# DLRM tower on one core: weight loads of the cross stage moved from SyncE's queue to ScalarE's

## The reference, cut to what matters

```python
q1, q2 = attention_pool(x, w1, b1, w2), attention_pool(x, w3, b3, w4)     # softmax over the 50 fields
h = concat([q1, q2]) @ w5 + b5                                            # 300 numbers
f6 = h @ w6 + b6
iu, ju = triu_indices(300, k=1)                                           # 44850 pairs
f7 = (h[:, iu] * h[:, ju] * g) @ w7 + b7                                  # w7 is 44850 x 300: the cross stage
out8 = concat([f6, f7]) @ w8 + b8
z = einsum('bu,bku->bk', out8, label_embedding)                           # 200 dot products a row
y = relu(relu(concat([z, dense_ctx]) @ W_top1 + b1) @ W_top2 + b2) @ W_top3
```

## Time and profile before

| | |
|---|---|
| median of 3 runs | 1852.51 us (1850.72 to 1853.8) |
| the profiled execution | 1854.63 us, its span 1852.8 us |
| TensorE busy | 1690.2 us, 91% of the span |
| VectorE busy | 1666.4 us, 90% |
| ScalarE busy | 1028.8 us, 56% |
| GpSimd busy | 554.8 us, 30% |
| moved by DMA | 561.70 MB, 303 GB/s on the mean |
| granted TensorE clock | 0.963 of full speed |

### The profile page before, as it was taken

How to read it: one execution, slowest core, us unless ns; L and a number is a source line. 1 busy time by engine, 2 the same in 40 slices (tenths; PEclk the granted TensorE clock), 3 DMA queues, 4 the chain that set the end, 5 groups by cost and what they waited for, 6 DMA issues and landing times.

```text
span 1852.8 us, 26080 instructions
## 1 busy us (share of the span) xinstructions
PE 1690.2 (91%) x7084; PEld 1249.0 (67%) x7084; DVE 1666.4 (90%) x5850; ACT 1028.8 (56%) x3233; POOL 554.8 (30%) x413
## 2 busy tenths in 40 slices
PE   2788899999999999999999999999997999998751
PEld 1555567777777777777777777777775777775531
DVE  5998979989999889999999999999998888867676
ACT  3786684684466644466654664456653544454434
POOL 7777506827300135400077018500000000000053
PEclk8899999999999999999999999999998999998975
DMA  9488955757988688989768766997649999989975
GB/s 277 114 290 316 340 181 189 244 169 278 380 320 308 238 325 350 353 333 342 288 223 337 272 253 216 385 418 295 247 163 396 421 390 378 401 311 419 420 304 242
DMA packets 97054, 561.70 MB, mean 303 GB/s; under 512 B 15567, under 2 KB 15941, under 8 KB 71309
## 3 DMA queue, kind: packets, MB, share of 16 engines
q1 hardware_dynamic: 77629, 498.39, 69.7%
q0 software_dynamic: 19264, 61.64, 10.5%
q10 hardware_dynamic: 16, 0.00, 0.0%
HBM read 559.98 MB, written 0.00 MB: 302 GB/s over the span
## 4 chain that ended last, share of the span: by engine, by line
PE 54%; DVE 23%; DMA 10%; POOL 6%; issue 4%; ACT 2%; SPq 0%; DVEq 0%; ACTq 0%; POOLq 0%
PE acc L1000 47%; DVE junk L618 11%; DMA w_sb<-in_w 8%; DVE qa L660 6%; DVE prod L770 6%; POOL x L561 4%; PE coarse L849 2%; DMA lab<-in_labels 2%; POOL lab L561 2%; PE acc L915 1%; PE misc L922 1%; PE acc L896 1%; PE acc L899 1%; ACT waste L1120 1%; PE acc L881 1%
## 5 line engine op out<-in xcount | busy, mean ns | idle before, releaser
L1000 PE MATMUL acc<-w_sb,prod 128*128 128x300 f32 (+2 forms) x5648 | 1528.1, 421 | 58.8 <-DMA w_sb<-in_w 41.3
L1000 PEld LDWEIGHTS acc<-w_sb,prod 128*128 128x128 f32 (+2 forms) x5648 | 1043.2, 192 | 405.7 <-DMA w_sb<-in_w 51.8
L1225 ACT ACTIVATE prod<-prod,g_all 128x256 f32<-128x256 f32 (+4 forms) x1615 | 686.3, 470 | 465.9 <-DVE prod L770 463.5
L561 POOL DMA_INDIRECT x<-in_tbl,ids_sb x368 | 477.7, 1298 | 664.9 <-DVE qa L660 558.9
L770 DVE TENSOR_TENSOR prod<-fine,coarse 128x1280 f32<-128x1280 f32 (+4 forms) x325 | 423.3, 1308 | 102.9 <-PE coarse L849 100.9
L618 DVE SCALAR_TENSOR_TENSOR junk<-lab,heads 128x300 bf16<-128x300 f32 x1208 | 477.6, 461 | 12.7 <-DMA lab<-in_labels 12.2
L618 DVE SCALAR_TENSOR_TENSOR junk<-x,heads 128x300 bf16<-128x300 f32 x1128 | 445.2, 461 | 24.0 <-DMA x<-in_tbl,ids_sb 23.9
L660 DVE SCALAR_TENSOR_TENSOR qa<-x,ex,qa 128x300 f32<-128x300 f32 x612 | 275.6, 523 | 0.0
L592 POOL TENSOR_TENSOR x<-x,out 128x2400 f32<-128x2400 f32 x5 | 26.2, 5253 | 599.9 <-ACT out L1095 591.1
L1120 ACT ACTIVATE waste<-x 128x300 bf16<-128x300 f32 x368 | 161.8, 440 | 26.4 <-DMA x<-in_tbl,ids_sb 25.1
L1044 ACT ACTIVATE picked<-hh 128x256 f32<-128x256 f32 (+4 forms) x325 | 121.6, 375 | 0.0
(11 more groups left out here) (107 smaller groups left out, 518.9 us busy)
## 6 DMA issues: line engine op xcount, KB each, us to landing
w_sb<-in_w SPq DMA_DIRECT2D x320, 750.0 KB, 6.6
lab<-in_labels SPq DMA_DIRECT2D x146, 1200.0 KB, 8.6
x<-in_labels SPq DMA_DIRECT2D x54, 1200.0 KB, 9.8
x<-in_tbl,ids_sb POOLq DMA_INDIRECT x368, 5.4
w_sb<-in_w SPq DMA_DIRECT2D x5, 450.0 KB, 3.7
prod<-in_v_i SPq DMA_DIRECT2D x1, 710.0 KB, 4.7
prod<-in_v_j SPq DMA_DIRECT2D x1, 710.0 KB, 7.1
w_sb<-in_w SPq DMA_DIRECT2D x1, 703.1 KB
```

The lines of the kernel that those rows point to most:

```text
L561: pool.indirect_dma_start(out=row_of(t, n), out_offset=None, in_=tables[n], in_offset=bass.IndirectOffsetOnAxis(ap=ids_sb[:, t, n:n + 1], ...
L1000: last = pe.matmul(acc[:, t % 3, 0:EMB], prod[0:rows, u % RING, m, t % 2 * P:(t % 2 + 1) * P], w7_sb[0:rows, u % W7_RING, m * EMB:(m + 1) ...
L1225: act.activation(chunk, chunk, ACT.Copy, scale=g_all[0:rows, pair:pair + 1]).then_inc(chunk_ready, 1)
```

## The change

The w7 loads of units 4 to 324 leave SyncE's list and are issued by ScalarE, on ScalarE's queue, one in each unit u from 2 to 322, right after the scaling of that unit's last chunk, for unit u + 2. Their wait (unit n - 4 used) goes with them. SyncE issues the first four w7 loads and then the slabs alone, in the same order among themselves, each with the wait it had. The sizes, `W7_RING` and `SLOTS` are as they were.

```diff
             for kind, n in LOADS:
                 if kind == "w7":
-                    if n >= W7_RING:
-                        sp.wait_ge(unit_used, n - W7_RING + 1)
-                    width = chunks_of(n) * EMB
-                    sp.dma_start(w7_sb[:, n % W7_RING, 0:width], w7[n % UNITS][:, 0:width]
-                                 ).then_inc(w7_loaded[n % W7_RING], 16)
+                    if n < W7_RING:
+                        sp.dma_start(w7_sb[:, n, :], w7[n]).then_inc(w7_loaded[n], 16)
                     continue
...
+            def load_w7(n):
+
+                width = chunks_of(n) * EMB
+                act.wait_ge(unit_used, n - W7_RING + 1)
+                act.dma_start(w7_sb[:, n % W7_RING, 0:width], w7[n % UNITS][:, 0:width]
+                              ).then_inc(w7_loaded[n % W7_RING], 16)
+
...
                     if m == 1 and u + RING < TOTAL:
                         pick_window(u + RING)
+                    if m == FINE - 1 and W7_RING <= u + 2 < TOTAL:
+                        load_w7(u + 2)
                     tick = u * FINE + m
```

## The result

The changed kernel takes 1855.97 us (median of 20 runs, 1852.52 to 1858.61), the kernel before 1853.18 (20 runs, 1849.52 to 1856.28). The ratio is 1.0017, with a 95% interval of 1.0010 to 1.0024. The forecast was 9.6 us faster. The predicted time of 1843 is 13 us off: the measured one lies above the forecast's own range of 1836 to 1850 and just inside the wide one of 1829 to 1857. The spans of the two profiled executions are 1856.2 and 1852.8 us, so the traces show about the same difference, 3.4 us.

The account below looks back on a forecast made before the run. TensorE (54% of the chain) and VectorE (23%) were taken to share the bound, with late data in places. Terms summed to -10.1, rounded to -9.6 from 1854.6: 1845.0, so median 1843; own range 1836 to 1850, wide 1829 to 1857.

Parts of the forecast that it names:

- the end stretch: Last cross units, DMAs full from 1645 to 1770 us: order of bytes changes nothing; 0, bounds -5 and +5.
- unit 247: Burst of six slabs: TensorE's 9.73 us wait for w7 shrinks, later slab 110 takes part back; -3.5, bounds 0 and -12.
- Unit 37: Four slabs ahead of w7: on its own queue w7 takes what gathers took, the 7.4 us wait goes; -8.
- (a): Head, 160 to 200 us: w7 beside the four earlier slabs lands late at two or three pairs; +1.5, bounds 0 and 6.
- (b): Around unit 37: four w7 issues by ScalarE, 0.33 us each, lie on the path; +1.3.
- The 2.4 us wait: One more TensorE wait for a w7 load behind a slab goes; -2.4.
- Elsewhere: Other units: w7, issued about one unit ahead, can be late behind a slab or two; +1, bounds 0 and 4.
- the change brings nothing: Rival, whole kernel: same bytes on the same engines, slabs lose what w7 gains; 1852.5 us, give or take 2; chance 0.20.

Follow-up runs that it names:

- late33: The changed kernel with slab 0 also waiting until unit 32 is used, so slabs 0 to 3 go out near 210 us: 1854.9 us, ratio 1.0016.
- order110: The changed kernel with slabs 110 and 111 issued ahead of the six slabs 112 to 117: 1843.1 us, ratio 0.9959.
- short_lead: The kernel before, one queue, with w7 of unit n also waiting until unit n - 2 is scaled, as late as in the change: 1875.2 us, ratio 1.0129.
- swap: Against the changed kernel, queues exchanged: SyncE issues w7 up to four units ahead, ScalarE most slabs, slabs 0 to 3 at units 33 to 36: 1875.1 us, ratio 1.0125.
- before_order: The kernel before, one queue, slabs 110 and 111 ahead of the six, those one behind each w7 of units 249 to 254: 1859.8 us, ratio 1.0045.
- one_queue: The kernel before with only its list reordered: slabs 0 to 3 later, 110 and 111 earlier, 112 onwards paced from unit 249: 1834.6 us, ratio 0.9898.

## Why the prediction was wrong, step by step

Three steps failed: the end stretch, put at 0 (+5.9), unit 247, put at -3.5 (+0.8), and the w7 loads beside the slabs in the head, put at +1.5 (the head lost 3.8 to 6.4, ScalarE's issues included). The rest held within 2 us.

- **Unit 37, -8**: right in size. The stage 36 to 45 is 8.3 us shorter. But by late33 the cause isn't the queue alone, since 5.2 us of waits stay beside the burst: the wait went mostly because the slabs moved off. The premise that w7 on its own queue takes what the gathers took, 7.1 to 9.1 us, failed there (up to 11.6): a gather moves 0.15 MB, a w7 load 0.77.
- **(a), +1.5 with bounds 0 and 6, and (b), +1.3**: under-sized. Unit 36 starts 6.4 us late (its cross 3.8 to 6.4 over the three traces with this head), and late33, with the slabs at 210, has its cross 0.7 late. The mechanism and the place were right: the first load beside a slab took 10.8 us from issue to landing where 7.1 are free. I took 8 at two or three pairs; four landings of 9.2 to 10.8 came with the first slab alone, beside the gathers and in a stretch already at 0.97. ScalarE's issue is 334 ns, as taken; that four of them lie on the path at unit 37 no run shows.
- **The 2.4 us wait**: measured -4.3, since the wait of before had also cost clock: 0.93 was granted in 1015 to 1040 before, 1.00 after. Before, then after:

```profile
1015.00:1040.00 25.00, 22.63 (x93) 16.67 (x92) 23.38 (x96) 14.34 (x47) 4.49 (x5) 0.93 0.87 346
```

```profile
1015.00:1040.00 25.00, 25.00 (x110) 18.93 (x109) 25.00 (x105) 19.98 (x66) 2.91 (x4) 1.00 0.92 344
```

- **Unit 247, -3.5 with bounds 0 and -12**: this step failed: +0.8. That slab 110 stays behind the six and holds VectorE was foreseen; its size was wrong. It took 20.1 us from issue to landing before and 25.9 after, 5.8 more instead of the 3.1 that I set. I had w7 of units 248 to 250 pass slab 110, "of which about two did not before". By the landings none did before, as they stood behind it in the queue (w7 248 landed at 1418.4, slab 110 at 1416.6), and all three do now (1404.9, 1409.6 and 1415.4 against 1418.6): 2.3 MB, 5.4 us at the 425 GB/s of that stretch, and the rate was 423 before (windows 1392.7 to 1418.6 and 1396.4 to 1416.5). And 3.1 was compared with absolute times: all of it came 3.7 us earlier in the changed kernel, so TensorE's 5.7 at unit 249 hold only 2.0 of gain from this place, and the next unit none. That unit 249 starts at 1423.9, close to the forecast 1424.9, is luck: the 3.7 were gained elsewhere. order110 shows that the 12 were there for another order. The three w7 loads in the changed kernel, and slab 110:

```profile
L1049 ACTq DMA_DIRECT2D w_sb<-in_w x3: 334/335/335, 1394.1 to 1406.2; - x3
...
DMA to landing us min/median/max: 9.1/10.7/11.0
```

```profile
L547 SPq DMA_DIRECT2D lab<-in_labels x1: 328/328/328, 1392.7 to 1392.7; - x1
...
DMA to landing us min/median/max: 25.9/25.9/25.9
```

- **The end stretch, 0 with bounds -5 and +5**: this step failed most: +5.9. "An order of bytes changes nothing where all of them are needed" left out that they needn't be moved inside the stretch. By the packets in the trace, the changed kernel enters unit 288 with one w7 load less landed (0.77 MB) and has 0.4 slabs more landed at unit 324: 55.0 MB instead of 53.8, or 2.9 us at 413 GB/s. The other 3.0 are rate, 404 against 413 GB/s, lost in the last 13.6 us: SyncE waits for free places there, and the DMAs run short. The windows of before, then after:

```profile
1640.20:1760.00 119.80, 100.10 (x387) 69.09 (x388) 89.71 (x368) 62.90 (x224) 0.00 (x0) 0.94 1.00 413
1760.00:1770.50 10.50, 8.31 (x33) 5.56 (x32) 8.54 (x39) 3.82 (x13) 0.00 (x0) 1.00 1.02 416
```

```profile
1637.40:1760.00 122.60, 96.90 (x386) 65.57 (x387) 90.02 (x366) 63.06 (x224) 0.00 (x0) 0.99 1.00 412
1760.00:1773.60 13.60, 8.90 (x34) 5.76 (x33) 9.62 (x45) 4.05 (x14) 0.00 (x0) 1.00 0.84 332
```

The step put this whole term at nothing. short_lead (one queue, short lead: 135.9) loses as much, with one w7 load more in the stretch, 0.2 slabs fewer, and 400 GB/s; swap (two queues, long lead: 137.5) loses as much with no w7 load more, 0.5 slabs more, and 396. So either half of the change costs about all of it, and the two don't add up. The three kernels with one queue and the long lead (before, before_order, one_queue) all have 413 or 414 GB/s and 130 us there. Why the rate falls in the others is open.
- **Elsewhere, +1**: +2.4 in 190 to 246. It isn't w7 that is late there but slabs: VectorE's waits for them in 1160 to 1225 went from 4.0 to 6.7 us.

```profile
DVE junk L615 <- DMA lab<-in_labels: 6.7, 6, 2.8
```

The steps summed to -10.1 and the trace has +3.4. The 13.5 between are 3.3 in the head (with unit 37), 4.3 at unit 247, 5.9 in the end stretch, 1.4 elsewhere and 0.5 in stages that no step named, less 1.9 at unit 180. It came out closest to the rival *the change brings nothing*, and in kind by its mechanism: w7 gains and the slabs lose. But the rival had no loss in the end stretch, the largest after the head's. The Trainium skill's rule (DMA: Bandwidth & Descriptors, section "Issuing engines are not separate DMA queues"), that DMAs of several issuers interleave on the same engines and only issue time is saved, gave the right time. It gives no place: no issue time was on the path, and the time is level because 12.6 us of gains at units 37 and 180 met 15.5 of losses in four other stretches, which is luck.

## What to carry to other kernels

A queue of its own takes a load out of line, but all that stood in line with it is let loose too: price what the others will now collide with, and what holds them back. Try the order first: another order in the list of the one queue, with no new queue, gave 18.6 us here. Where DMAs are full and then idle, a prefetch with a long lead is the thing to hold back; five slabs of 1.2 MB each were worth some 6 to 8 us in three pairs of kernels (6.5, 7.6 and 5.9).

## What the runs showed of the hardware that I had not expected

- A slab's sixteen completion signals don't come together, and VectorE starts 0.02 us after the last. By the semaphore events slab 110's came from 1414.93 to 1416.55 us before and from 1416.74 to 1418.62 in the changed kernel, the last of them 0.8 us behind the fifteenth. A slab that is alone in its queue lands 0.3 to 0.7 us after its last packet ends with one queue (13 slabs of the kernel before) and 0.3 to 1.0 with two (12 slabs of the changed kernel).
- A second queue doesn't move more. With both busy (and gathers beside them in the first window) the DMAs carried 396 to 399 GB/s in 160 to 200, 424 in 1396 to 1411 and 414 in 1645 to 1770, with one queue 423 and 417 in the last two.
- A w7 load on its own queue isn't served first. In the changed kernel's end stretch slabs 166 to 181, nearly always two outstanding, land in 8.3 to 10.1 us and w7 loads of units 293 to 324, three or four outstanding, in 8.5 to 15.1.
